# Taking the first page of a second expert from eight tiles, and splitting the weights of two experts once, in a graph layer with a mixture of experts

## The reference, cut to what matters

```python
# graph stage: x (2048, 512), adj (2048, 2048), weight (512, 512)
s = relu(matmul(quant(layernorm(x)) , quant(weight)))       # 4 and 3 bit steps
x = x + matmul(adj / a, quant(s)) * a * step
# expert stage: 16 experts, the two best for each token
xf = layernorm(x)
probs = softmax(xf @ Wr + br)                                # (2048, 16)
w, idx = top_k(probs, 2);  w = w / w.sum()
h = gelu(layernorm(xf @ W1[e] + b1[e]) * g1[e] + be1[e])     # 512 -> 512
y[token] += w * (h @ W2[e] + b2[e])                          # for both experts e of a token
out = x + y
```

## Time and profile before

| | us |
|---|---|
| median of three runs (511.26 to 513.44) | 511.75 |
| the profiled execution's own time | 510.59 |
| its span | 508.8 |
| PE busy | 466.0 (92%) |
| DVE busy | 353.1 (69%) |
| ACT busy | 289.3 (57%) |
| POOL busy | 236.4 (46%) |

### The profile page before, as it was taken

The page is one execution under the profiler, slowest core; times in us unless marked ns, Lnnn a source line. Parts: engine busy times, 40 slices in busy tenths (PEclk is TensorE's granted clock), DMA queues, the critical chain, the costliest instruction groups (busy, mean ns, idle before and its releaser), DMA issues. The chain is left out here.

```text
span 508.8 us, 10186 instructions
## 1 busy us (share of the span) xinstructions
PE 466.0 (92%) x2297; PEld 382.8 (75%) x2298; DVE 353.1 (69%) x741; ACT 289.3 (57%) x474; POOL 236.4 (46%) x269
## 2 busy tenths in 40 slices
PE   0799999999999999677999999999999999999970
PEld 0578888878888887566888888888787887888850
DVE  5898864846689777967766686676887766786410
ACT  1666543543454533446667667668777865776440
POOL 4354420521464526546444555554545454555531
PEclk9999999999999999769999999999999999999995
DMA  8621232675796641135887776957778788464433
GB/s 298 255 84 48 77 104 84 237 228 186 260 304 247 201 154 43 46 100 192 234 250 166 215 202 136 249 107 217 236 236 255 235 276 210 93 149 73 82 49 41
DMA packets 31403, 87.25 MB, mean 171 GB/s; under 512 B 6000, under 2 KB 6144, under 8 KB 30864
## 3 DMA queue, kind: packets, MB, share of 16 engines
q1 hardware_dynamic: 17504, 56.54, 33.8%
q0 software_dynamic: 9264, 22.02, 21.2%
q10 hardware_dynamic: 4608, 8.39, 4.4%
HBM read 67.79 MB, written 19.14 MB: 171 GB/s over the span
## 5 line engine op out<-in xcount | busy, mean ns | idle before, releaser
L694 POOL DMA_INDIRECT xg<-xn_rows,tok_i x39 | 49.1, 1259 | 85.9 <-ACT gate L953 72.1
L975 ACT ACTIVATE g_sb<-ps,be_sb,g_sb 128x128 f32<-128x128 f32 x152 | 57.2, 457 | 50.9 <-PE ps L1745 50.9
L1406 DVE TENSOR_TENSOR w_lo<-w_raw,w_hi x58 | 68.3, 1219 | 8.7 <-issue 8.7
L719 POOL DMA_INDIRECT out<-y_sb,scat_i x35 | 60.8, 1738 | 23.0 <-DMA out<-y_sb,scat_i 12.9
L1413 DVE TENSOR_SCALAR h_hat<-ps,h_mv,h_rs 128x512 f32<-128x512 f32 x38 | 30.7, 808 | 47.1 <-issue 28.4
L783 ACT ACTIVATE adj_hi<-adj_raw,small 128x1024 fp32r<-128x1024 f32 x32 | 36.8, 1150 | 44.7 <-PE ps L1520 38.8
L946 ACT ACTIVATE w_hi<-w_raw x29 | 54.9, 1914 | 3.7 <-DMA w_raw<-in_w 2.4
L1083 DVE SCALAR_TENSOR_TENSOR adj_lo<-adj_raw,small,adj_hi 128x1024 fp32r<-128x1024 f32 x32 | 40.7, 1272 | 22.4 <-ACT adj_hi L783 22.3
L623 POOL TENSOR_SCALAR rstd<-mv 128x1 f32<-128x1 f32 x15 | 14.6, 976 | 76.1 <-DVE mv L1129 76.1
L1520 PE MATMUL ps<-sup,adj_hi 128*128 128x512 f32 x192 | 49.1, 398 | 0.0
L1520 PE MATMUL ps<-sup,adj_lo 128*128 128x512 f32 x192 | 49.1, 398 | 0.0
(11 more groups left out here) (215 smaller groups left out, 963.0 us busy)
## 6 DMA issues: line engine op xcount, KB each, us to landing
w_raw<-in_w SPq DMA_DIRECT2D x64, 512.0 KB
adj_raw<-in_adj_steps SPq DMA_DIRECT2D x32, 512.0 KB, 3.3
out<-x_sb ACTq DMA_DIRECT2D x16, 256.0 KB, 2.8
xn_rows<-xn ACTq DMA_DIRECT2D x16, 256.0 KB, 2.3
x_sb<-in_x SPq DMA_DIRECT2D x3, 1024.0 KB, 12.5
gw_raw<-in_gnn_w SPq DMA_DIRECT2D x1, 1024.0 KB, 5.0
x_sb<-in_x SPq DMA_DIRECT2D x2, 512.0 KB, 6.9
xg<-xn_rows,tok_i POOLq DMA_INDIRECT x39, 4.3
```

Source lines behind the costliest of these rows:

```text
L694: return pool.indirect_dma_start(to[:, s % 2, :], None, xn_rows, bass.IndirectOffsetOnAxis(ap=tok_i[:, s:s + 1], axis=0)).then_inc(landed[ ...
L719: pool.indirect_dma_start(out, bass.IndirectOffsetOnAxis(ap=at, axis=0), y_sb[:, par, :], None, compute_op=ALU.add).then_inc(scattered[par ...
L975: ins = act.activation(g_sb[:, par, c * P:(c + 1) * P], ht_ps(par)[:, c * P:(c + 1) * P], ACT.Gelu, scale=g1_sb[:, bass.ds(e_s * C + c, 1) ...
L1406: ins = dve.tensor_tensor(w_lo[:, n, at], w_raw[:, n, :, :].rearrange("p a n -> p (a n)")[:, at], w_hi[:, n, at].bitcast(F32), ALU.subtract)
```

## The change

Page 0 of expert 1 is also taken after eight tiles: `early_pad` and `early_tokens` treat experts 0 and 1, POOL gathers a second page into `xg0`, and this is the loop's slot 0, run by the ordinary slot steps but with its transposes and layer 1 (`first_layer_1`, `_lo`, `_end`) ahead of the last table. Slot 1 is page 1 of expert 0. The plan's masks are changed for that order (`ahead`, a 17th column). One buffer `w_split` holds hi and lo of both layers for two experts from the graph stage on; `e_w` and the second split are gone, and expert 1's layer 2 is split in the seam (`early_hi(1, 1)` on ACT, four `early_lo` on DVE behind the plan). The weights are loaded two windows earlier, the hit buffers are rearranged in three sets (HIT_SET), and other buffers and PSUM banks are moved. On PE, rank(3), the wait for e_x_lo and finish_t(14) stand between the last two half steps; early layer 1 is one piece; the early hidden transposes and the first half of early layer 2 stand ahead of the last table, the second half behind compact. The bias product takes two rows of `bias_row` instead of 128, since other buffers now lie in the rest. SP's load of expert 2 waits for the first gate too. POOL gathers slots 1 to 3 after tok_i.

```diff
+HIT_SET = (0, 0, 0, 1, 2)
+PART_AT = ((1, 2), (0, 3))
...
-EARLY_ROWS_AFTER = 45
+EARLY_ROWS_AFTER = 43
 EARLY_TILES = 8
-EARLY_HI_IN = {13: 0, 17: 1}
-EARLY_LO_IN = {13: (0, 0), 14: (0, 1), 15: (0, 2), 17: (0, 3), 20: (1, 0), 21: (1, 1), 23: (1, 2)}
-EARLY_PAD_IN, EARLY_TOKENS_IN = 16, 21
+EARLY_HI_IN = {11: (0, 0), 13: (0, 1), 15: (1, 0)}
+EARLY_LO_IN = {11: (0, 0, 0), 12: (0, 0, 1), 13: (0, 0, 2), 14: (0, 0, 3), 15: (0, 1, 0), 16: (0, 1, 1), 17: (0, 1, 2),
+               18: (0, 1, 3), 20: (1, 0, 0), 21: (1, 0, 1), 22: (1, 0, 2), 23: (1, 0, 3)}
+EARLY_PAD_IN, EARLY_TOKENS_IN = 16, 20
 HITS_IN = {10: (0, 2), 11: (0, 3), 12: (0, 4), 13: (0, 5), 14: (0, 7), 15: (0, 8),
            16: (1, 3), 17: (1, 5), 18: (1, 6), 19: (1, 8), 22: (2, 2), 23: (2, 4)}
...
+NO_WORD = sum((E - 2) << FIELD * i for i in range(5))
+BIAS_OUT_IN, WEIGHTS_IN = 6, 8
...
-    put("least", P * np.where(np.arange(E) == 0, 2, 1)[None, :])
+    put("least", P * np.where(np.arange(E) < 2, 2, 1)[None, :])
...
-    begin = (p % PAGES)[:, None] == np.where(mine == 0, 1, 0)
-    starts = begin * (mine < E - 1)
-    put("word_of", np.concatenate([mine - (E - 1) + E * starts, mine - (E - 1), begin], 1))
+    begin = page == np.where(mine < 2, 1, 0)
+    starts = begin * (mine > 0) * (mine < E - 1)
+    put("word_of", np.concatenate([mine - (E - 1) + E * starts, mine - (E - 1), begin + ahead - 1], 1))
...
+
+        where[0] = w_at
+        w_split = place("w_split", [P, 2 * 4 * C * D], F32R)
...
-        w_hi = place("w_hi", [P, 2, 2 * C * D], F32R)
-        w_lo = place("w_lo", [P, 2, 2 * C * D], F32R)
...
+        def w_part(n, low, e, c):
+
+            at = PART_AT[n][low] * (C * D) + c * D
+            return w_split[:, e % 2 * (4 * C * D) + at:e % 2 * (4 * C * D) + at + D] if isinstance(e, int) else \
+                w_split[:, bass.ds((e & 1) * (4 * C * D) + at, D)]
...
-            return ps[:, 2 + par, :]
+            return ps[:, 4 - par, :]
...
-            return ps[:, 4 + par, :]
+            return ps[:, 2 + 3 * par, :]
...
             sp.wait_ge(x_tp, 2)
+            sp.wait_ge(gate_ok, 1)
...
-                if b >= 2 and not first:
-                    pool.wait_ge(table_mm, b - 1)
+                if b in (1, 2):
+                    pool.wait_ge(table_mm, b)
+                if b >= 3:
+                    pool.wait_ge(adj_mm, STEPS + WINDOWS + 1)
                 for j in range(first, last):
...
                                         bass.IndirectOffsetOnAxis(ap=e_tok[:, 0:1], axis=0)).then_inc(e_in, 16)
+                pool.indirect_dma_start(xg0[:, :], None, xn_rows[0:EARLY_TILES * P, :],
+                                        bass.IndirectOffsetOnAxis(ap=e_tok[:, 1:2], axis=0)).then_inc(first_in[0], 16)
 
...
             last_rstd(T - 1)
-            row_hits(3, 0, 6)
+            row_hits(3, 0, 3)
+            early_rstd()
+            row_hits(3, 3, 6)
             dense_gates(3)
             dense_gates(4)
             row_hits(4, 0, 2)
...
-            act.wait_ge(adj_mm, STEPS + WINDOWS + 1)
             act.wait_ge(small_in, 64)
-            split(0, 0, 48)
             act.wait_ge(xn_ok, T)
             store_xn(T - 1)
             finish_t(T - 1)
-            split(0, 1, 96)
+            slot_x_hi(0, 0)
+            slot_gate(0, 0, 1)
+            early_h_hat()
             gate_exp(4)
             act.preload_act_table(ACT.Gelu)
+            early_gelu()
             act.wait_ge(table_mm, 4)
             act.activation(tab_rows[:, :], table_ps, ACT.Copy).then_inc(tab_rows_ok, 1)
+            early_hi(1, 1)
             act.wait_ge(table_mm, len(BATCHES))
             act.activation(tab_sb[:, :, :], table_t_ps, ACT.Copy).then_inc(tab_ok, 1)
-            early_h_hat()
-            early_gelu()
-            split(1, 0, 48)
...
-            split_next(0, expert_in(word, 1), starts_in(word, 1))
...
             add_br(T - 3)
             pick(3)
             choose(3)
+            val_hits(2, 4, 6)
+            find(3)
+            gate_values(3)
+            link(dve.memset(pages_f[:, 1, E:E + 1], float(P)))
             add_tile(T - 1)
-            find(3)
+            val_hits(3, 0, 3)
             norm_last(T - 1)
             add_br(T - 2)
-            val_hits(2, 4, 6)
-            val_hits(3, 0, 6)
+            early_stats()
+            val_hits(3, 3, 6)
             add_br(T - 1)
             pick(4)
             choose(4)
-            gate_values(3)
+            slot_x_lo(0, 0)
             gate_values(4)
-            early_stats()
             find(4)
...
             ins.then_inc(sel_ok, 1)
-            early_lo(1, 3)
-            for piece in range(C):
-                split_piece(0, 0, piece, 1)
+            early_g_lo()
 
             dve.wait_ge(compact_mm, 1)
             dve.tensor_scalar(tok_i[:, :], compact_ps, -1.0, 0.0, ALU.add, ALU.max).then_inc(tok_ok, 1)
             link(dve.tensor_scalar(dumps[:, :], compact_ps, 0.0, const("dump_row_1"), ALU.is_equal, ALU.mult))
-            dve.scalar_tensor_tensor(scat_i[:, :], compact_ps, -1.0, dumps[:, :], ALU.add, ALU.add)
+            dve.scalar_tensor_tensor(scat_i[:, :], compact_ps, -1.0, dumps[:, :], ALU.add, ALU.add).then_inc(scat_ok, 1)
             link(dve.tensor_scalar(used_i[:, :], pl[:, 4:5], 4.0, None, ALU.subtract))
             dve.tensor_scalar(pairs[:, :], used_i[:, :], 1, None, ALU.arith_shift_right)
+            slot_stats(0, 0)
             dve.wait_ge(words_mm, 1)
...
-            link(dve.tensor_scalar(fields[:, :], words_ps, 0.0, None, ALU.add))
+            link(dve.tensor_scalar(fields[:, :], words_ps, 1.0, None, ALU.add))
...
-            slot_x_lo(0, 0)
-            slot_x_lo(1, 1)
             dve.wait_ge(table_ok, 1)
             word = load_plan(dve, 0)
             rest = dve.value_load(pairs[0:1, 0:1], min_val=E // 2 - 2, max_val=SLOTS // 2 - 2)
-            slot_stats(0, 0)
-            split(1, 0, 1)
             slot_h_hat(0, 0)
+            slot_x_lo(1, 1)
+            for piece in range(C):
+                early_lo(1, 1, piece)
             slot_x_lo(2, 0)
             slot_stats(1, 1)
-            split_next(0, expert_in(word, 1), starts_in(word, 1))
...
+            def bias_product(dst, n, row):
+
+                pe.matmul(dst, two_rows[0:2, :], bias_row[n][0:2, row], start=True, stop=False)
+
...
+            def first_layer_1():
+
+                pe.wait_ge(split_hi[0], 2)
+                pe.wait_ge(x_hi_ok, 1)
+                bias_product(h_ps(0), 0, slice(D, 2 * D))
+                first_part(xt_hi, 0)
+
+            def first_layer_1_lo():
+
+                pe.wait_ge(split_lo[0], 2)
+                first_part(xt_hi, 1)
+
+            def first_layer_1_end():
+
+                pe.wait_ge(x_lo_ok, 1)
+                first_part(xt_lo, 0, last=True).then_inc(mm1, 1)
...
                 if hs == EARLY_ROWS_AFTER:
                     early_rows()
-            pe.wait_ge(e_x_lo_ok, 1)
-            finish_t(T - 2)
-            rank(3)
+                if hs == 2 * WINDOWS - 2:
+                    rank(3)
+                    pe.wait_ge(e_x_lo_ok, 1)
+                    finish_t(T - 2)
             router(T - 2)
+            pe.wait_ge(rows_ok, 1)
             early_layer_1()
             finish_t(T - 1)
-            early_layer_1_lo()
+            pe.wait_ge(logits_ok, T - 1)
+            rows_t(0, 0, 16)
             router(T - 1)
-            early_layer_1_end()
+            first_layer_1()
             table(2)
+            early_hidden()
+            first_layer_1_lo()
+            rank(4)
             table(3)
-            rank(4)
+            first_layer_1_end()
+            early_layer_2()
             pe.wait_ge(tab_rows_ok, 1)
-            pe.wait_ge(acc_read, T)
...
             ins.then_inc(compact_mm, 1)
-            pe.wait_ge(e_h_hat_ok, 1)
+            early_layer_2_end()
+            pe.wait_ge(scat_ok, 1)
...
+            def layer(dst, n, s, par, e, act_hi, act_lo, lo_ok, done):
+
+                pe.wait_ge(split_hi[n], e + 1)
+                bias_product(dst, n, bass.ds((e & 3) * D, D))
...
             def layer_2(s, par, e):
-                if isinstance(s, int) and s == 0:
-                    pe.wait_ge(e_y_ok, 1)
...
             def hidden_t(s, par):
 
+                if isinstance(s, int) and s == 1:
+                    pe.wait_ge(e_y_ok, 1)
                 pe.wait_ge(h_hat_ok, s + 1)
...
-            early_hidden()
-            early_layer_2()
-            pe.wait_ge(tok_ok, 1)
-            rows_t(0, 0, 16)
             rows_t(1, 1, 16)
-            layer_1(0, 0, 0)
             pe.wait_ge(table_ok, 1)
             word = load_plan(pe, 0)
             rest = pe.value_load(pairs[0:1, 0:1], min_val=E // 2 - 2, max_val=SLOTS // 2 - 2)
+            layer_1(1, 1, expert_in(word, 1))
             rows_t(2, 0, 16)
-            layer_1(1, 1, expert_in(word, 1))
             slot(0, 0, None, expert_in(word, 2), 16)
             slot(1, 1, expert_in(word, 0), expert_in(word, 3), 32)
```

(49 more changed lines are left out.)

281 lines of the change are left out of this document (119 added, 162 removed).

## The result

The changed kernel takes 532.48 us (median of 4 runs, 531.84 to 536.67); the kernel before, on the same chip, 511.81 (4 runs). The ratio is 1.0416, 95% interval 1.0357 to 1.0475: slower by 4.2%. The profiled execution took 531.84 us with a span of 529.9. The forecast was 506.2 with a range up to 514.0.

What follows compares the result with a forecast made beforehand. TensorE's own instruction stream bounds both stages, leaving the seam between them: +3.75 - 2.86 - 3.1 - 5.5 + 1.5 + 0.7 = -5.5 us from 510.59, 505.1; as median 506.2. Range 500.5 to 514.0.

Steps and rivals of the forecast that it cites:

- Part 7: Bias products over 2 rows instead of 128, 76 places in the loop: taken as 0, between -7 and +25 us.
- hidden 1: Transposes of slot 1's hidden rows on TensorE, at 240.54 before, forecast at 233 to 235; the loop runs gapless after.
- rival (d): TensorE runs empty around each two-row bias product: 0.16 us each, 12.2 us, time 518.4; chance 0.12.
- sign of being wrong: The prediction is wrong if a loop slot takes longer than 6.9 us, or hidden 1 comes after 238.
- Part 1: Around the last half step: last tile starts later, TensorE waiting 2.7 us for rank(3), then a clock fall; +3.75 us.
- A: The moment the last tile is added on VectorE: 199.36 before, forecast 203.1.
- Part 2: From the last tile's add to tok_i, 18.76 us before: less work and waiting ahead, full clock; -2.86 us.
- Part 3: From tok_i to the first transposed rows: slot 1's gather comes first, 4.5 us instead of 7.6; -3.1 us.
- Part 4: First rows to hidden 1, 14.83 us before: slot 0's work and idles leave, -5.5; a second clock fall, +1.5.
- Part 5: Inside the loop: early scatter and scatters 0 to 2 run one after another, delaying h_hat(5); +0.7 us, bounds 0 and 4.
- Part 6: Graph-stage windows: extra w_lo pieces, a Copy, earlier tables, tokens and weights, covered by VectorE's lead of about 4 us; nothing.
- the sum: All terms from the seam and loop added: -5.5 us; the bias products count 0 in it.

## Why the prediction was wrong, step by step

**The step that failed is Part 7, the bias products: "I take 0".** It measured +24.4 us in the changed kernel from hidden 1 to the end, and +28.0 alone. What the runs show fits the mechanism of rival (d), given 0.12, whose price was too small as well: 0.16 for running empty once, where 0.37 was measured, gaps on both sides of the product and a slower group behind. The upper bound in Part 7, "twice, +25", was the right size, but rival (d) and the range were built on the lower figure. The value was chosen by the row of the same instruction with 128 rows, which is nearest in form but differs in just what the edit changed. On an engine that is busy 99.88 of 100 us, 0.07 us an instruction decided the sign, and the text itself said so. Its own sign of being wrong, a slot longer than 6.9 us, came true with 7.57; from the bias product to the next pass 0.43 us, not 0.32.

**Part 1, A +3.75.** Measured +4.9, by the mechanism forecast, in all its steps: rank(3) waited (2.7 forecast), the clock fell, and half step 47 ran at half speed. Its size was short by 1.2 us, most of it because half step 47 started at 200.79 and not near 199.9. TensorE, then VectorE, of the changed kernel (compare):

```profile
199.73 0.29 PE L1571 MATMUL ps<-first_r,ones_r 128*128 128x48 f32 x1 [2.93 <-DVE so_far L1188]
...
200.79 3.38 PE L1521 MATMUL ps<-sup,adj_lo 128*128 128x512 f32 x8
```

```profile
204.29 0.75 DVE L1128 SCALAR_TENSOR_TENSOR x_sb<-ps,small,x_sb 128x512 f32<-128x512 f32 x1 [2.46 <-PE ps L1521]
...
220.72 0.22 DVE L1381 TENSOR_SCALAR tok_i<-ps 128x54 int32<-128x54 f32 x1 [0.41 <-PE ps L1733]
```

The half-microsecond stretches that answer to the earlier trace rows have two short falls, 3.4 us each, in place of one of 13.6:

```profile
200.50:201.00 0.50, 0.50 (x5) 0.50 (x4) 0.43 (x3) 0.00 (x0) 0.04 (x1) 0.50 0.00 0
...
203.50:204.00 0.50, 0.50 (x3) 0.43 (x2) 0.00 (x0) 0.00 (x0) 0.00 (x0) 0.90 0.00 0
...
227.50:228.00 0.50, 0.50 (x2) 0.09 (x2) 0.50 (x2) 0.00 (x0) 0.00 (x0) 0.50 0.60 189
```

**Part 2, A to tok_i -2.86.** Measured 16.65 us, -2.1: right in kind; 0.7 short. VectorE reached find(4) 10.7 us after the last tile's add (214.99 less 204.29), not 10.1, which is most of it; with 128 rows it took 10.3.

**Part 3, tok_i to the first rows -3.1.** Measured 4.2 us (4.5 forecast), -3.4.

**Part 4, first rows to hidden 1, -5.5 and +1.5.** Measured 12.04 us, -2.8. The second fall came where forecast. Mis-sized was x_hi(1), which TensorE waited for 1.5 us and not 0.8, and both layers paid for their two-row products (the same stretch took 11.62 us with 128 rows). TensorE:

```profile
225.16 0.66 PE L1662 MATMUL ps<-k_sb,xg 128*128 128x128 f32 x4 [1.97 <-DMA xg<-xn_rows,tok_i]
227.33 0.66 PE L1615 MATMUL ps<-bias_row,two_rows 2*128 x1 [1.52 <-ACT xt_hi L930]
227.92 2.07 PE L1749 MATMUL ps<-w_split,xt_hi 128*128 x4
```

Hidden 1 moved by +4.9 - 2.1 - 3.4 - 2.8 = -3.3 (rounded) and not by -6.2. It stands at 237.20, behind the 233 to 235 that the prediction named, but not behind the 238 of its sign of being wrong.

**Part 5, scatters +0.7.** Right as a mechanism. GpSimd did wait for its own scatters ahead of scatters 0 and 1 (compare):

```profile
247.01 1.63 POOL L740 DMA_INDIRECT out<-y_sb,scat_i  x1 [3.30 <-DMA out<-e_xg,e_tok]
...
254.26 1.60 POOL L740 DMA_INDIRECT out<-y_sb,scat_i  x1 [2.68 <-DMA out<-y_sb,scat_i]
```

In the changed kernel the longer slots hid it: price 0. With 128 rows it showed as 0.61 us ahead of hidden 5; two later waits of TensorE add 0.7. So slower products had covered waits, which is part of why taking them out gave 22 us and not the 24.4 that the loop had lost.

**Part 6, at nothing.** Right: 60.00 of 60 us in the windows.

**What is left without Part 7.** The changed kernel with 128 rows took 510.16, 2.4 us under the kernel before, where the sum promised 5.5. In the two profiles hidden 1 came 4.2 us earlier (236.35; 234.3 by the sum, so 2.0 are missing there), and from there to the end 3.6 us were lost, where the sum had 0.7. Of these, 1.6 lie behind the last slot's hidden rows, where the clock fell over layer 2 (it didn't in the profile of the kernel before), 0.7 in the first two slots, 0.8 at hidden 5 with its wait, and 0.5 in later slots. The two profiled executions lie only 0.5 us apart where the medians lie 2.4: that of the kernel before (510.59) was 2.0 us below the median it is compared with.

## What to carry to other kernels

On the bound engine, an edit to an operand's shape is a change to every instance of the instruction: where no row shows the new shape, its price belongs in the range at its full bound, or is measured first. In a stream of products over 128 rows like this one, a short one is best padded with zeros to more than 64 rows, or short ones are put side by side so that the passage is paid once. And a wait moved to another place may bring its fall of the clock with it; filling it with products is a separate edit.

## What the runs showed of the hardware

- A product of 512 columns (fp32r, the rounded float32 of the kernel) over 2 or 64 rows between products over 128 costs 0.36 or 0.35 us more in the loop than one over 65 (0.01) or 128, at a granted clock of 1.00; two of 256 columns in a row cost it once (538.80 us against 540.58).
- The weight load of a two-row product takes no longer (182 ns against 190), but the loads stand idle 13.4 us in all ahead of the 76 of them, against 2.1, and the load behind it starts with its own product (301.56) where it started 0.23 us ahead.
- In the changed kernel and its forms with 128 rows, each fall of the clock between the graph stage and the last products lay in or a few microseconds behind a wait of TensorE of 1.5 us or more. Such a wait is neither enough nor needed: the wait of 1.9 us at the last slot of the kernel before was followed by no fall (the one of 1.8 with 128 rows was), nor was the one of 2.04 ahead of table(3) in three profiles of four; and in the kernel before with 2 and with 64 rows the clock fell near 203.3, where TensorE's longest wait since 190 us had been 0.63 us, and stayed low for 6.8 and 3.4 us. With 65 and with 128 rows it didn't fall there.
- Filled with products whose results nothing uses, the waits of the seam were followed by no fall in three profiles of three; those of the last slot in two of two.
